# One transposition of 128x16 and four transfers for a unit's maxima, in place of four transpositions of 128x4 and one transfer

## Chip, cores and metric

The kernel runs on one core of one Trainium2 chip. The metric is the device time of one execution in microseconds; lower is better.

## What is computed

A gated block: 1024 query tokens (2 batches of 512, width 128) attend in 16 heads of 64 to 32 context tokens and to themselves, and a feed-forward layer of 8 experts follows, each token weighted to two of them. Only the attention matters here, cut to its core:

```
xn = layernorm(ctx, ...);  ln = layernorm(latents, ...)
q  = ln @ Wq
kv = concat([xn @ Wkv, ln @ Wkv])
qn = rmsnorm(q) * scale;   kn = rmsnorm(k)
sim  = einsum('bhid,bhjd->bhij', qn, kn)       # 544 keys a query: 32 context, 512 latents
attn = softmax(sim)                            # row maximum subtracted
out  = einsum('bhij,bhjd->bhid', attn, v) @ Wout + bout
```

## The kernel before

The attention is done in 8 **units** (u = 0 to 7), each one batch and a group of HG = 4 heads. A unit has 8 **slots**, so n = 0 to 63; slot n computes the turned scores (keys on partitions, 512 queries on the free axis) of one head and two of the four key tiles. Every engine has its own program, written out by slots from FIRST = -4 to LAST = 68, and semaphores join them. Numbers are kept in high and low halves of 16 bits, so most products come in pairs or triples.

Three things are needed of a unit before its slot 8u can start. (1) The **stacks** W1 and W2 (two buffers each, by u % 2): query and key halves laid one above the other, copied from HL by eight transfers on SyncE (L406 to L415) at slot 8u - 8, after the products of slot 8u - 9 or, for u = 1, at once. (2) The row **maxima**: score(j) on TensorE (L1381) computes the scores once with queries on partitions, VectorE reduces them to negated maxima (L991), joins them with the context's (L1072) and writes nm16, 128 queries on partitions by 4 query tiles and 4 heads. (3) The maxima must lie on the four partitions DH to M_ROWS = 64 to 67 of W2, one row a head, because the product of L1527 subtracts them by contracting with a one-hot block there. To get there, in slot 8u - 3 (nm_at) TensorE transposes nm16 into the bank o_ps[0] (turn_maxima, L1412), ScalarE copies it to nmT in SBUF (turned_maxima, L699), and in SyncE's slot 8u - 2 one transfer (L434) spreads nmT over the four places of the heads in W2. For unit 0 the same is done in the start-up. TensorE's slot 8u waits for w2_ok, sh_ok (the transfer of the maxima) and w1_ok.

SyncE's program between two units is: the maxima's transfer of unit u (slot 8u - 2), the eight transfers of the stacks of unit u + 1 (slot 8u, after the scores of slot 8u - 1), then for each of four heads three transfers of **pc_st** (L388, slot 8u + 1), which bring the context's exponentials of unit u into place; TensorE's times_values needs those of head 0 in slot 8u + 3 (L1362 with vst). SyncE further issues the experts' weights, 1 MB each: gate weights at slot 46 (L442) right behind unit 6's maxima, down weights at 51 (L445), up weights at 54 (L451) right behind unit 7's maxima. In the start-up SyncE issues unit 0's stacks, the maxima of unit 0, vst (six transfers, after vc), the stacks of unit 1 and pc_st of unit 0. ScalarE casts the experts' weights in quarters in slots 49 to 60 (SPLIT_AT: gate in 49 to 52, down in 53 to 56, up in 57 to 60).

Within a slot TensorE does the turned scores (L1526, L1527), one score(j) for a later unit, the projection and transposition of a later unit's query or key tile, the products with the values of slot n - 2 (times_values, L1356, L1357, L1362), and then, where it is due, turn_maxima. Unit 7 and half of 6 have projections of the output (L1333, L1316) in place of tiles.

Of the kernel before, what the change touches and what calls it, by code (L numbers as in the profile page):

```python
# [5 lines left out]
P = 128  # L6
F32 = mybir.dt.float32
F32R = mybir.dt.float32r
F16 = mybir.dt.float16
# [12 lines left out]
def flamingo_gated_block(nc, x, ctx_in, mask, g_xattn, g_ffn, ln_x_g, ln_x_b, ln_l_g, ln_l_b, qn_g, kn_g,  # L22
                         Wq, Wkv, Wout, bout, router, w_gate, w_up, w_down, out):
    B, N, D = x.shape
# [4 lines left out]
    HG = 4  # L29
# [13 lines left out]
    with ExitStack() as ctx:  # L43
# [79 lines left out]
        Vst = sb("vst", [3 * C, B, H, DH + 1], F16)  # L123
        nm_main = sb("nm_main", [P, 2, HG, QT], F32)
        nm16 = sb("nm16", [P, QT, HG], F16)
        nmT = sb("nmT", [HG, QT, P], F16)

        NP = 4
        p = [sb(f"p{k}", [P, 1024], F32) for k in range(NP)]
# [229 lines left out]
        @block.sync  # L359
        def _(sp):  # L360
            x_v = x.rearrange("b (t p) d -> p (b t) d", p=P)
            sp.dma_start(x_sb[:, 0:QT, :], x_v[:, 0:QT, :]).then_inc(x_in, 16)
            wq_v = Wq.rearrange("d (g c) -> d g c", g=NG)
            wkv_v = Wkv.rearrange("d (k g c) -> d k g c", k=2, g=NG)
            w_v = wqkv.rearrange("p (g k c) -> p g k c", g=NG, k=3)
            sp.dma_start(w_v[:, 0, 0, :], wq_v[:, 0, :]).then_inc(w0_in, 16)
            sp.dma_start(w_v[:, 0, 1:3, :], wkv_v[:, :, 0, :]).then_inc(w0_in, 16)
            sp.dma_start(x_sb[:, QT:T, :], x_v[:, QT:T, :]).then_inc(x_in2, 16)
            sp.dma_start(w_v[:, 1:NG, 0, :], wq_v[:, 1:NG, :]).then_inc(w_in, 16)
            sp.dma_start(w_v[:, 1:NG, 1, :], wkv_v[:, 0, 1:NG, :]).then_inc(w_in, 16)  # L370
            sp.dma_start(w_v[:, 1:NG, 2, :], wkv_v[:, 1, 1:NG, :]).then_inc(w_in, 16)
            for k, g in enumerate((qn_g, kn_g)):
                for r in range(2):
                    sp.dma_start(qk_gains[DH * r:DH * (r + 1), k:k + 1], g.unsqueeze(1)).then_inc(qkg_in, 16)
            sp.dma_start(mask_u8[:, :], mask.rearrange("b c -> (b c)").unsqueeze(0)).then_inc(mask_in, 16)
            for h in range(HG):
                sp.dma_start(mask_cu[C * h:C * (h + 1), :], mask.rearrange("b c -> c b"),
                             allow_slow_non_contiguous=True).then_inc(mask_in, 16)
            sp.dma_start(bout_b[:, :], bout.partition_broadcast(P)).then_inc(rest_in, 16)
            sp.dma_start(wr[:, :], router).then_inc(rest_in, 16)  # L380
            sp.dma_start(wout[:, :, :], Wout.rearrange("(c p) d -> p c d", p=P)).then_inc(rest_in, 16)

            def stack(u, h):

                for k, part in enumerate((pc_hi, pc_hi, pc_lo)):
                    if h == 0 and k == 2:
                        sp.wait_ge(cplo_ok, u + 1)
                    sp.dma_start(pc_st[u % 2][C * k:C * (k + 1), h, :], part[C * h:C * (h + 1), :]).then_inc(pcst_ok[h], 16)  # L388

            def slot(n):  # L390
                if n - 1 in cst_at:
                    u = cst_at[n - 1]
                    need(sp, pv_ok, 8 * (u - 1))
                    sp.wait_ge(cexp_ok, u + 1)
                    for h in range(HG):
                        stack(u, h)
                if n in W_AT:
                    u = W_AT[n]

                    need(sp, st_ok, 8 * (u - 1))  # L400
                    need(sp, cst_ok, u - 1)
                    sp.wait_ge(hi_ok, QT * (u + 1))
                    w1, w2, hl = W1[u % 2], W2[u % 2], HL[u % 2]
                    for odd in range(2):
                        rows = slice(DH * odd, DH * (odd + 1))
                        sp.dma_start(w1[0:DH, :, odd, :], hl[rows, 0, :, :]).then_inc(w1_ok[u % 2], 16)  # L406
                        sp.dma_start(w1[DH:P, 0:2, odd, :], hl[rows, 0, 0:2, :]).then_inc(w1_ok[u % 2], 16)
                    need_lo(sp, QT * (u + 1))
                    for odd in range(2):
                        rows = slice(DH * odd, DH * (odd + 1))  # L410
                        sp.dma_start(w1[DH:P, 2:4, odd, :], hl[rows, 1, 2:4, :]).then_inc(w1_ok[u % 2], 16)
                    for odd in range(2):
                        rows = slice(DH * odd, DH * (odd + 1))

                        sp.dma_start(w2[0:DH, :, odd, :], hl[rows, :, :, :].rearrange("p a c n -> p (a c) n")[:, 2:6, :]  # L415
                                     ).then_inc(w2_ok[u % 2], 16)
                if n == FIRST:
                    sp.wait_ge(cklo_ok, 1)
                    for odd in range(2):
                        rows = slice(DH * odd, DH * (odd + 1))  # L420
                        for k, part in ((K1c[0:DH], 0), (K1c[DH:P], 1), (K2c[0:DH], 0)):
                            sp.dma_start(k[:, :, odd, :], kc_hl[rows, part, :, :]).then_inc(kc_ok, 16)
                if n == -1:
                    sp.wait_ge(const_z, 4)
                    sp.wait_ge(cvlo_ok, 1)
                    for b in range(B):
                        for k, cols in enumerate((slice(0, DH + 1), slice(DH + 1, VW), slice(0, DH + 1))):
                            sp.dma_start(Vst[C * k:C * (k + 1), b, :, 0:cols.stop - cols.start],
                                         vc[b * C:(b + 1) * C, :, cols]).then_inc(vbd_ok, 16)
                if n - 1 in nm_at:  # L430
                    u = nm_at[n - 1]
                    sp.wait_ge(nmc_ok, u + 1)

                    sp.dma_start(W2[u % 2][DH:M_ROWS, 2:4, :, :].rearrange("p a e n -> p (a e) n"),  # L434
                                 nmT[:, :, :].rearrange("p q c -> p (q c)").unsqueeze(1).broadcast_to([HG, HG, N])
                                 ).then_inc(sh_ok[u % 2], 16)

                if n == 46:
                    sp.wait_ge(w2_ok[0], 32 * (UNITS // 2))
                    sp.wait_ge(w1_ok[0], 96 * (UNITS // 2))  # L440
                    sp.wait_ge(s_ok, 8 * (UNITS - 1))
                    sp.dma_start(wg.rearrange("p (e f) -> p e f", e=E), w_gate.rearrange("e d f -> d e f")).then_inc(wg_in, 16)  # L442
                if n == 51:
                    sp.wait_ge(pv_ok, 8 * 6)
                    sp.dma_start(wd.rearrange("p (e c d) -> p e c d", e=E, c=FC),  # L445
                                 w_down.rearrange("e (c p) d -> p e c d", p=P)).then_inc(wd_in, 16)
                if n == 54:
                    sp.wait_ge(w2_ok[1], 32 * (UNITS // 2))
                    sp.wait_ge(w1_ok[1], 96 * (UNITS // 2))
                    sp.wait_ge(s_ok, 8 * UNITS)  # L450
                    sp.dma_start(wu.rearrange("p (e f) -> p e f", e=E), w_up.rearrange("e d f -> d e f")).then_inc(wu_in, 16)  # L451

            for n in range(FIRST, LAST):
                slot(n)
            out_v = out.rearrange("b (t p) d -> p (b t) d", p=P)
            for half in range(B):
                if half == 0:
                    sp.wait_ge(yp_ok, E)
                else:
                    sp.wait_ge(y_ok, E * QT)  # L460
                sp.dma_start(out_v[:, half * QT:(half + 1) * QT, :], x1[:, half * QT:(half + 1) * QT, :]).then_inc(out_ok, 16)
            sp.wait_ge(out_ok, 16 * B)
# [185 lines left out]
        def _(act):  # L648
# [46 lines left out]
            def turned_maxima(u):  # L695
                act.wait_ge(nmT_ok, u + 1)
                if u:
                    act.wait_ge(sh_ok[(u - 1) % 2], 16 * ((u - 1) // 2 + 1))
                nc.scalar.copy(nmT[:, :, :], o_ps[0][0:HG, 0:256].bitcast(F16).rearrange("p (q c) -> p q c", c=P)  # L699
                               ).then_inc(nmc_ok, 1)  # L700

            weights_hi(0)
            act.wait_ge(gains_in, 16 * 4)
# [567 lines left out]
        def _(pe):  # L1271
# [136 lines left out]

            def turn_maxima(u):
                pe.wait_ge(nm_ok, u + 1)  # L1410
                for q in range(QT):
                    last = nc.tensor.transpose(o_ps[0][0:HG, 64 * q:64 * (q + 1)].bitcast(F16), nm16[:, q, :],  # L1412
                                               ident_h[:, :])
                last.then_inc(nmT_ok, 1)

            pe.wait_ge(wlo_ok, 1)
            pe.wait_ge(lnlo_ok, 2)
# [92 lines left out]
            def turned_scores(n):  # L1510
                u, h, i = n // 8, n % 8 // 2, n % 2
                if n % 8 == 0:
                    pe.wait_ge(w2_ok[u % 2], 32 * (u // 2 + 1))
                    pe.wait_ge(sh_ok[u % 2], 16 * (u // 2 + 1))
                    pe.wait_ge(w1_ok[u % 2], 96 * (u // 2 + 1))
                if n == 0:
                    pe.wait_ge(onehot_ok, 2)
# [177 lines left out]
```

## Time and profile before

| | |
|---|---|
| three runs | 346.26 us median, 345.56 to 347.9 |
| the profiled execution | 347.66 us, of which its span 345.9 us |
| TensorE busy | 301.0 us, 87% of the span |
| VectorE, GpSimd, ScalarE busy | 79%, 78%, 59% |
| granted TensorE clock, mean of the span | 0.975 |

Up to about 55 us the kernel starts up (norms, weights split into halves, the first two units' queries and keys); 55 to about 260 us are the slots; from there to the end the experts run, paced by GpSimd. A view of the trace gives times in us from the start of the span. PE is TensorE, PEld its weight loads, DVE VectorE, ACT ScalarE, POOL GpSimd, SP SyncE; a q behind a name is the engine's own sequencer, which issues transfers. L numbers are lines of the kernel. Durations of matrix products overlap, since they are pipelined.

### The profile page before, as it was taken

To read this page: it belongs to the slowest core of one execution; us is meant where nothing else is said; L and a number is where in the kernel's file an instruction comes from. 1 tells how busy PE (TensorE), PEld (TensorE's weight loads), DVE (VectorE), ACT (ScalarE), POOL (GpSimd) and SP (SyncE) were. 2 spreads that over 40 slices of the span, in tenths; PEclk is the share of its full clock that TensorE was granted. 3 is DMA by queue.
4 is the path that set the end of the run, shared out by engine and by line. 5 is a ranking of instruction groups with operands and counts; after the bars stand their busy time and mean duration, and the time that the engine had idled before them with its cause. 6 is when DMAs were issued, how large, how long until landed. Compare 5 with 4: busy or idle time off the path is not lost.

```text
span 345.9 us, 8714 instructions
## 1 busy us (share of the span) xinstructions
PE 301.0 (87%) x3321; PEld 184.3 (53%) x3321; DVE 273.5 (79%) x515; ACT 204.9 (59%) x357; POOL 268.0 (78%) x203
## 2 busy tenths in 40 slices
PE   0566578789999999999999999999987898988992
PEld 0233243446555555555555656788764674654652
DVE  3898878958899899898988976955647885887994
ACT  2463746727756757665766656467662657554551
POOL 8689896866999999999989987565971475875562
PEclk9996969989999999999999999999999999999999
DMA  6505322810712614416307259450100000001001
GB/s 165 151 1 127 69 35 44 193 39 17 174 45 49 152 36 107 106 23 148 69 20 164 60 154 181 112 165 9 38 2 3 2 1 0 2 3 31 2 0 33
DMA packets 33708, 23.63 MB, mean 68 GB/s; under 512 B 10818, under 2 KB 33154, under 8 KB 33666
## 3 DMA queue, kind: packets, MB, share of 16 engines
q1 hardware_dynamic: 32722, 23.03, 28.8%
q8 instruction: 27, 0.44, 0.6%
q10 hardware_dynamic: 944, 0.04, 0.2%
q14 instruction: 15, 0.12, 0.1%
HBM read 5.87 MB, written 0.52 MB: 18 GB/s over the span
## 4 chain that ended last, share of the span: by engine, by line
PE 53%; POOL 16%; issue 11%; ACT 5%; DVE 5%; SPq 4%; DMA 4%; POOLq 0%; DVEq 0%; ACTq 0%
POOL p_lo L628 9%; PE big L1526 7%; PE big L1527 7%; PE o_ps L1362 5%; PE big L1381 5%; PE o_ps L1356 4%; PE o_ps L1357 4%; DMA pc_st<-pc_lo 3%; PE tv L1369 3%; POOL rms_r L492 3%; PE pj L1333 2%; PE pj L1292 2%; PE pj L1293 1%; PE pj L1294 1%; POOL x_sb L641 1%
## 5 line engine op out<-in xcount | busy, mean ns | idle before, releaser
L593 POOL TENSOR_TENSOR p_lo<-p 128x1024 f16<-128x1024 f32 x64 | 121.8, 1915 | 13.1 <-ACT p L792 13.1
L792 ACT ACTIVATE p<-big 128x1024 f32<-128x1024 f32 x64 | 65.6, 1025 | 48.9 <-PE big L1527 48.8
L991 DVE TENSOR_REDUCE nm_main<-big 128x2 f32<-128x1024 f32 x64 | 78.2, 1222 | 18.1 <-PE big L1381 17.3
L492 POOL TENSOR_TENSOR rms_r<-meansq,power 128x8 f32<-128x8 f32 x32 | 52.3, 1637 | 16.1 <-DVE meansq L965 16.1
L628 POOL TENSOR_TENSOR p_lo<-p,p_lo 128x512 f16<-128x512 f32 x32 | 37.0, 1158 | 25.9 <-ACT p_lo L865 25.9
L1526 PE MATMUL big<-w 128*128 128x512 f16 x128 | 48.8, 381 | 1.9 <-ACT p L792 1.6
L1527 PE MATMUL big<-w 68*128 68x512 f16 x128 | 48.7, 380 | 0.0
L1356 PE MATMUL o_ps<-v,p 128*128 128x65 f16 x512 | 40.7, 194 | 0.0
L1357 PE MATMUL o_ps<-v,p 128*128 128x64 f16 x512 | 40.6, 195 | 0.0
L1356 PEld LDWEIGHTS o_ps<-v,p 128*128 128x128 bf16 x512 | 35.9, 99 | 6.7 <-issue 3.6
L1357 PEld LDWEIGHTS o_ps<-v,p 128*128 128x128 bf16 x512 | 34.4, 98 | 3.2
L860 ACT ACTIVATE p<-big 128x512 f32<-128x512 f32 x32 | 19.1, 598 | 23.4 <-PE big L1617 23.3
L1381 PE MATMUL big<-hl 64*128 64x512 f16 x128 | 25.8, 400 | 5.8 <-DVE nm_main L991 4.9
L1236 DVE SCALAR_TENSOR_TENSOR p<-p,big 128x512 f32<-128x512 f32 x32 | 21.9, 684 | 11.4 <-ACT p L860 10.9
L1636 PE MATMUL o_ps<-wd_hi,p_lo 128*128 128x128 f16 x128 | 23.2, 220 | 6.4 <-POOL p_lo L628 6.4
L1362 PE MATMUL o_ps<-v,p_lo 128*128 128x65 f16 x512 | 26.1, 194 | 0.0
L965 DVE TENSOR_REDUCE meansq<-squares 128x8 f32<-128x512 f32 x32 | 21.9, 683 | 5.4 <-ACT squares L670 4.7
L1615 PE MATMUL big<-x2T_hi,gu_hi 128*128 128x512 f16 x64 | 24.3, 379 | 2.0 <-DVE p L1240 2.0
L1617 PE MATMUL big<-x2T_hi,wqkv_hl 128*128 128x512 f16 x64 | 24.3, 379 | 0.0
L1616 PE MATMUL big<-x2T_lo,gu_hi 128*128 128x512 f16 x64 | 24.3, 379 | 0.0
L1381 PEld LDWEIGHTS big<-hl 64*128 64x128 f16 x128 | 6.2, 93 | 32.8 <-issue 25.5
L1640 PE MATMUL o_ps<-wd_hi,p_lo 128*128 128x128 f16 x128 | 23.1, 219 | 0.0
(228 smaller groups left out, 715.6 us busy)
## 6 DMA issues: line engine op xcount, KB each, us to landing
w<-hl SPq DMA_DIRECT2D x32, 256.0 KB, 4.2
w<-hl SPq DMA_DIRECT2D x32, 128.0 KB, 3.7
pc_st<-pc_hi SPq DMA_DIRECT2D x64, 32.0 KB, 1.9
pc_st<-pc_lo SPq DMA_DIRECT2D x32, 32.0 KB, 1.9
hl<-n_kernel_gating_EDF_dram SPq DMA_DIRECT2D x1, 1024.0 KB, 6.5
hl<-L_ffn_kernel_up_EDF_dram SPq DMA_DIRECT2D x1, 1024.0 KB, 5.5
o_sb<-in_L_xattn_Wkv_dram SPq DMA_DIRECT2D x2, 384.0 KB, 7.2
x_sb<-in_x_dram SPq DMA_DIRECT2D x2, 256.0 KB, 3.7
```

What stands on the lines that cost most here:

```text
L492: nc.gpsimd.tensor_tensor(rms_r[:, tau % QT, :], meansq[:, tau % QT, :], power[:, 0:8], ALU.pow).then_inc(rr_ok, 1)
L593: nc.gpsimd.tensor_tensor(p_lo[m % NP][:, :], p[m % NP][:, :], p_hi[m % NP], ALU.subtract).then_inc(plo_ok, 1)
L628: nc.gpsimd.tensor_tensor(hid_lo[m % NH], hid[m % NH], hid_hi[m % NH], ALU.subtract).then_inc(hlo_ok, 1)
L792: nc.scalar.activation(p[n % NP][:, :], st_ps, ACT.Exp).then_inc(exp_ok, 1)
L991: nc.vector.tensor_reduce(nm_main[:, u % 2, 2 * c:2 * c + 2, q], s2_ps.rearrange("p (k n) -> p k n", k=2), AX_X, ALU.max, negate=True).the ...
L1356: nc.tensor.matmul(o_of(q), ph[:, c], vh, start=start and q == 0, stop=False, skip_group_check=True)
L1357: nc.tensor.matmul(o_of(q)[:, 0:DH], ph[:, c], vl, start=False, stop=False, skip_group_check=True)
L1362: last = nc.tensor.matmul(o_of(q), pl[:, c], vh, start=False, stop=True, skip_group_check=True)
L1381: last = nc.tensor.matmul(s2_ps[:, 512 * r:512 * (r + 1)], HL[u % 2][rows, 0, c, q * P:(q + 1) * P], HL[u % 2][rows, 0, 2 + c, :], start=T ...
L1526: nc.tensor.matmul(o, w1[:, 2 + h // 2, h % 2, keys], w1[:, h // 2, h % 2, :], start=True, stop=False)
L1527: last = nc.tensor.matmul(o, w2[0:M_ROWS, h // 2, h % 2, keys], w2[0:M_ROWS, 2 + h // 2, h % 2, :], start=False, stop=True)
L1615: nc.tensor.matmul(o, gu_hi[k][:, w], x2T_hi[:, toks], start=True, stop=False)
```

## The change

A unit's maxima are turned by one transposition of 128x16 (128 queries by 4 tiles x 4 heads) into 16 partitions by 128 columns. ScalarE copies 16x128 in place of 4x512. The rows of query tile q now lie on partitions 4q to 4q + 3, while W2 wants all four tiles of a head on one partition, so SyncE issues four transfers, one a query tile, each with rows of 128 numbers (256 bytes) instead of 512 (1024 bytes). All waits on sh_ok count four times 16.

```diff
-        nmT = sb("nmT", [HG, QT, P], F16)
+        nmT = sb("nmT", [QT * HG, P], F16)
...
-                    sp.dma_start(W2[u % 2][DH:M_ROWS, 2:4, :, :].rearrange("p a e n -> p (a e) n"),
-                                 nmT[:, :, :].rearrange("p q c -> p (q c)").unsqueeze(1).broadcast_to([HG, HG, N])
-                                 ).then_inc(sh_ok[u % 2], 16)
+                    for q in range(QT):
+                        sp.dma_start(W2[u % 2][DH:M_ROWS, 2:4, :, q * P:(q + 1) * P].rearrange("p a e n -> p (a e) n"),
+                                     nmT[q * HG:(q + 1) * HG, :].unsqueeze(1).broadcast_to([HG, HG, P])
+                                     ).then_inc(sh_ok[u % 2], 16)
...
-                    act.wait_ge(sh_ok[(u - 1) % 2], 16 * ((u - 1) // 2 + 1))
-                nc.scalar.copy(nmT[:, :, :], o_ps[0][0:HG, 0:256].bitcast(F16).rearrange("p (q c) -> p q c", c=P)
-                               ).then_inc(nmc_ok, 1)
+                    act.wait_ge(sh_ok[(u - 1) % 2], 16 * QT * ((u - 1) // 2 + 1))
+                nc.scalar.copy(nmT[:, :], o_ps[0][0:QT * HG, 0:P // 2].bitcast(F16)).then_inc(nmc_ok, 1)
...
-                for q in range(QT):
-                    last = nc.tensor.transpose(o_ps[0][0:HG, 64 * q:64 * (q + 1)].bitcast(F16), nm16[:, q, :],
-                                               ident_h[:, :])
-                last.then_inc(nmT_ok, 1)
+                nc.tensor.transpose(o_ps[0][0:QT * HG, 0:P // 2].bitcast(F16), nm16[:, :, :].rearrange("p q h -> p (q h)"),
+                                    ident_h[:, :]).then_inc(nmT_ok, 1)
...
-                    pe.wait_ge(sh_ok[u % 2], 16 * (u // 2 + 1))
+                    pe.wait_ge(sh_ok[u % 2], 16 * QT * (u // 2 + 1))
```

On TensorE, in the start-up where unit 0's maxima are turned (between the transposition of a key tile and the projection of the context's values), the difference is this:

```order
 L1294 MATMUL pj<-wqkv_hl,lnT_lo 128x512
 L1369 MATMUL o_ps<-ident,qk 128x128 x4
-L1412 MATMUL o_ps<-ident_h,nm 4x128 x4
+L1411 MATMUL o_ps<-ident_h,nm 16x128
 L1292 MATMUL big<-wqkv_hl,lnT_hi 128x256
 L1293 MATMUL big<-wqkv_hl,lnT_hi 128x256
```

Four transpositions became one, in the same place; the same stands in each of the other seven units. On SyncE, in slots 46 to 48 (the maxima of unit 6, then the gate weights as hl, then the stacks of unit 7; lines behind 434 are numbered one higher after the change), it is this:

```order
 L388 DMA pc_st<-pc_hi 32x512 x2
 L388 DMA pc_st<-pc_lo 32x512
-L434 DMA w_0<-nmT 4x4x512
-L442 DMA hl<-L_ffn_kernel_gating_EDF_dram 128x8x256
+L435 DMA w_0<-nmT 4x4x128 x4
+L443 DMA hl<-L_ffn_kernel_gating_EDF_dram 128x8x256
 L406 DMA w_1<-hl 64x4x512
 L407 DMA w_1<-hl 64x2x512
```

The order of SyncE's transfers is kept; four issues stand where one stood, ahead of whatever follows.

## Rows read from the trace of the kernel before

**Rows 1.** The page: granted clock in 40 slices of 8.65 us; the chain by engine.

```profile
PEclk9996969989999999999999999999999999999999
...
PE 53%; POOL 16%; issue 11%; ACT 5%; DVE 5%; SPq 4%; DMA 4%; POOLq 0%; DVEq 0%; ACTq 0%
```

**Rows 2.** The chain in order of time, start-up: start us, us, what.

```profile
49.77 0.51 PE o_ps L1412 x4
...
51.68 0.21 PE big L1292
...
52.20 0.11 PE big L1292
...
54.94 0.65 SPq L428
...
55.64 0.63 SPq L428
...
67.76 2.95 DMA pc_st<-pc_lo
```

**Rows 3.** Waits of TensorE, whole span, then from 86 to 260 us: total, times, longest.

```profile
PE o_ps L1362 <- DMA pc_st<-pc_lo: 2.9, 3, 1.9
...
PE o_ps L1362 <- DMA pc_st<-pc_lo: 1.0, 2, 0.7
```

**Rows 4.** Busy time of each engine in the stretch 86 to 110 us.

```profile
86.00:110.00 24.00, 24.00 (x312) 13.93 (x309) 21.43 (x37) 15.84 (x26) 23.34 (x15) 1.00 0.38 84
```

**Rows 5.** The chain in unit 2: the four transpositions for unit 3.

```profile
128.36 0.32 PE o_ps L1412 x4
```

**Rows 6.** Lines 699 and 434 (duration min/median/max, first and last start); ScalarE's copies from PSUM.

```profile
L699 ACT COPY nmT<-o_ps x8: 557/574/575, 50.4 to 225.1; 4x512 f16<-4x512 f16 x8
...
L434 SPq DMA_DIRECT2D w<-nmT x8: 706/716/793, 51.0 to 225.7; - x8
...
L766 ACT COPY o_sb<-tv 128x512 f32<-128x512 f32 x16 | 9.4, 586 | 15.9 <-PE tv L1316 15.9
...
L693 ACT COPY p_lo<-o_ps 128x256 f32<-128x256 f32 x4 | 1.5, 372 | 0.0
```

**Rows 7.** Timeline of SyncE and TensorE, units 1 and 2; DMA rate in slices of 0.1 us from 105.

```profile
81.33 0.71 SPq L434 DMA_DIRECT2D w<-nmT  x1
...
86.22 0.38 PE L1526 MATMUL big<-w 128*128 128x512 f16 x1
...
105.14 0.71 SPq L434 DMA_DIRECT2D w<-nmT  x1
108.64 0.67 SPq L406 DMA_DIRECT2D w<-hl  x1
...
110.39 0.38 PE L1526 MATMUL big<-w 128*128 128x512 f16 x1
...
GB/s 0 0 0 0 0 0 0 0 0 0 0 0 0 0 10 20 31 31 20 21 21 10 82 0 0 0 0 0 0 0 0 0 0 0 0 0 0 0 0 0
```

**Rows 8.** The chain at unit 6's pc_st; line 388, durations of its issues.

```profile
212.93 4.25 DMA pc_st<-pc_lo
...
L388 SPq DMA_DIRECT2D pc_st<-pc_lo x32: 507/590/1937, 67.8 to 248.1; - x32
```

**Rows 9.** Timeline of SyncE and TensorE before unit 6.

```profile
201.25 0.72 SPq L434 DMA_DIRECT2D w<-nmT  x1
202.08 0.39 SPq L442 DMA_DIRECT2D hl<-n_kernel_gating_EDF_dram  x1
...
205.53 0.38 PE L1526 MATMUL big<-w 128*128 128x512 f16 x1
```

**Rows 10.** DMA busy tenths, 203 to 219 us (0.4 a slice), 248 to 252 (0.1), and its last landing.

```profile
DMA  3778999999999999999999999998841410303213
...
DMA  3630001640000561000000000000000000000000
...
pc_st<-pc_lo SPq DMA_DIRECT2D x1, 32.0 KB, 1.8
```

## Prediction

> **What bounds the kernel now.** I read the page's slices and its chain of work first, then the chain stretch by stretch, then SyncE's queue, because the change works on TensorE, ScalarE and SyncE together. The chain is 53% TensorE and 16% GpSimd; SyncE's queue has 4% and DMA 4% [rows 1]. By stretch it looks like this.
>
> From 49.77 to 70.84 us the start-up is bound first by TensorE (the four transpositions stand in it with 0.51 us), then by ScalarE and VectorE on vc, then by SyncE alone: fifteen transfers are issued one behind the other from 54.94 us, and the last thing waited for is the landing of the first head's pc_st [rows 2]. TensorE has then stood idle for 1.9 us, its longest wait for pc_st [rows 3]. From there to unit 6 TensorE is the bound: from 86 to 110 us it is busy 24.00 of 24.00 us, GpSimd 23.34 of them, VectorE 21.43 [rows 4]. A unit repeats every 24.17 us (slot 16's first product at 110.39, slot 8's at 86.22 [rows 7]). In unit 6 the chain leaves TensorE: it runs over SyncE's issues of pc_st and a landing 4.25 us after the third of them at 212.93 [rows 8]. The same happens more weakly in unit 7: of TensorE's three waits for pc_st, 2.9 us in all, two lie behind 86 us, with 1.0 us together and 0.7 the longer [rows 3]. Behind that come the experts, which the change does not touch.
>
> **What the change takes away.** (a) *Three of four transpositions per unit, on TensorE.* Four occupy 0.32 us of the chain in a full unit [rows 5]; they are pipelined, 0.08 us apart, so one leaves 0.08 and saves 0.24 us. In unit 0 four cost 0.51 us [rows 2], because the granted clock is still low there: the PEclk row reads 6 in the sixth slice, 43.2 to 51.9 us [rows 1], and products of 256 columns take 0.21 us up to 51.9 us, which is 1.2 GHz, and 0.11 us behind it, which is 2.4 GHz [rows 2]. One would save 0.38 us; but if the clock rises at the same instant as now, 0.38 us more of the work is done at half speed, and half the gain is given back. I take 0.3 us, bounds 0.2 and 0.4.
>
> (b) *ScalarE's copy.* It takes 574 ns for 4x512 [rows 6]. I have no 128-column copy from PSUM. A COPY of 512 columns takes 586 ns and one of 256 takes 372 ns, so 0.84 ns a column, and 128 columns would be 0.27 us; the bound from above is the 256-column copy itself. I take 0.27, by the slope of two rows of this operation: the copy ends 0.30 us sooner (0.20 at least). ScalarE is not in the chain here, so this is worth nothing by itself; it only brings the transfers forward. Together with (a) the first transfer is issued 0.54 us sooner.
>
> **What it adds.** (c) *Three more issues on SyncE per unit.* One nmT issue takes 716 ns [rows 6], and issues in a row stand 0.04 to 0.05 us apart [rows 2]. So the fourth is issued 3 x 0.76 = 2.28 us behind the first, and what SyncE does next can start 2.28 us later, less the 0.54 us. Where does that go?
> - Unit 0: the issue began at 51.0 us and took at most 0.79; SyncE then idled until 54.94 [rows 2, 6]. 3.1 us of cover against 1.7: nothing. Without that cover it would be 1.7 us straight on the chain, as everything from 54.94 to 67.76 us is SyncE issuing.
> - Units 1 to 5: unit 2's issue ended at 105.85, the next one (the stacks of unit 3) waits for slot 15's scores until 108.64 [rows 7]. Cover 2.79 against 1.7: nothing.
> - Unit 6: SyncE issues the 1 MB gate weights (L442) at 202.08, right behind nmT [rows 9]. They now go out at 202.08 - 0.54 + 2.28, so 1.74 us later against everything around. The stacks of unit 7 queue up behind them.
> - Unit 7: the up weights (L451) go out 1.7 us later, in slot 54, and are cast in slots 57 to 60 at the earliest, three slots of 3 us on. Nothing.
>
> (d) *The landing.* TensorE's first product of slot 8u waits for all four. No view gives a landing for nmT, so I work it out. In unit 2 packets flow at 10 to 31 GB/s in slices 15 to 22 of 0.1 us from 105.0 (the 82 GB/s in the next one I take for something else), which is 1.3 to 2.1 us after the issue [rows 7]. pc_st's semaphore comes 0.3 us behind its last packet (the last one is issued at 248.1, its packets run until 249.6, it lands after 1.8 [rows 8, 10]). So a transfer is there 2.4 us after its issue; a quarter of the bytes can shorten only the 0.7 us in which packets flow. The fourth lands 2.28 + 2.4 = 4.7 us behind the first issue, 4.2 if small packets are quick. Available are, from the first issue to the first product of the slot, 86.22 - 81.33 = 4.89 us in unit 1, 110.39 - 105.14 = 5.25 in unit 2 (and 5.24 in 3 to 5), 205.53 - 201.25 = 4.28 in unit 6 [rows 7, 9], each plus the 0.30 us of the copy. So the slack is 0.5 us in unit 1, 0.85 in units 2 to 5, and -0.1 to +0.4 in unit 6. I take 0.05 us of waiting, in unit 6 alone. In unit 0 the wait may reach 0.3 us, but TensorE has 1.9 us to give away there [rows 3].
>
> Four transfers overlap in this sum. pc_st's are issued 0.63 us apart and its bursts in the DMA row lie 0.6 us apart too [rows 10], so they do. The Trainium skill (DMA: Bandwidth & Descriptors, Rules for kernel authors) speaks against the change: many small transfers should be coalesced into one large, since under 64 KB one pays mostly overhead. The same page's section Anatomy of one DMA gives about 2 us of fixed cost to each. By a reading in which that cost falls due four times in a row, the time would be the serial rival's below; by the row it falls due once.
>
> (e) *The gate weights in unit 6.* This is the term that I am least sure of. From 203.4 to 214.6 us the DMA engines read 7 to 9 tenths: the gate weights, then unit 7's stacks, then pc_st [rows 10]. The first head's pc_st ends behind that queue, at 217.18 us, and TensorE has then been idle 0.7 us [rows 3, 8]. If the queue starts 1.74 us later and nothing else gives, TensorE resumes 1.74 us later. But the row thins out at 214.6 us, 2.6 us before that landing, and single issues of pc_st stall, up to 1.94 us where 0.59 is usual [rows 8]; that tail need not move along. Bounds 0 and 1.74; I take 1.2, nearer to the full shift because the saturated stretch is four times as long as the tail.
>
> **The sum.** Unit 0: -0.3. Units 1 to 5, where TensorE is full: 5 x -0.24 = -1.2. Unit 6: its own 0.24 only lengthens its wait, +1.2 for (e), +0.05 for (d). Unit 7: -0.24. Together -0.5 us, on a profiled execution of 345.9 us of span and 347.66 us in all. The median of the three runs is 346.26, 1.4 below that execution; the difference goes onto the median: **345.8 us**.
>
> **Rivals.**
> - *The gate weights hide (0.10).* If (e) is 0, and the wait of 0.3 us in unit 7 goes too, -0.4 - 1.2 - 0.24 - 0.3 = -2.1: **344.1**. For it: the thin tail. Against it: eleven busy microseconds before.
> - *GpSimd takes over (0.14).* It is busy 23.34 of 24.00 us [rows 4], so only 0.66 us of air stands in a unit; the waits between it and TensorE could eat the 0.24 us. Then -0.3 + 1.2 - 0.2 is +0.7: **347.0**.
> - *Late staging, the slower side (0.06).* If a transfer of 256-byte rows needs over 3.3 us from issue to landing (5.25 + 0.30 - 2.28), slot 8u begins late in every unit, and TensorE has no slack to give back. At 4.3 us it is 1.0 us in units 2 to 5, 1.4 in unit 1 and 1.9 in unit 6: +7.3, so **353**. For it: single issues of up to 1.94 us occur [rows 8]; one of those among the four costs a unit up to 0.5 us. Against it: the packets of today are done 2.1 us after the issue.
> - *Serial transfers (0.02).* If each began when the one before had landed, the fourth would land 4 x 2.4 = 9.6 us behind the first issue, 4.1 us late in each of units 2 to 5, 4.4 in unit 1, 5.0 in unit 6: +25, **371**. The pc_st rows speak against it.
>
> My forecast keeps 0.68. **Range 343.9 to 348.6**: the low end is the first rival; the high end is (e) in full (+1.74 instead of 1.2), no gain by (a) in unit 0, GpSimd eating most of the five units, and one stall of SyncE of 0.7 us between 54 and 68 us, where it is the chain. About 1% (3.5 us) is what a measurement of this kernel can tell from no change. Faster by more than that needs 342.8, which the first rival would have to overshoot: 0.02, taken from it. Slower needs 349.7, which only the last two reach: 0.08. Same keeps 0.90.
>
> **What would show it.** (a) one transposition of 128*16, 0.08 us in the chain, units 24.17 - 0.24 = 23.9 us apart (slot 16 less slot 8, first products). (b) the copy near 270 ns. (c) four issues 0.76 us apart, no later start of the stacks except in unit 6, where L443 comes 2.8 us behind nmT's first. (d) no DMA named as what ended an idle time before the first product of slots 8, 16, 24, 32, 40. (e) TensorE's wait for pc_st in unit 6 grows from 0.7 to about 2.1 us. I am wrong if that wait stays where it is, if the unit's period stays at 24.17, or if the first product of slot 8u waits for w.

## The result, and the profile after

The changed kernel takes 348.90 us (median of 20 runs, 345.18 to 351.0), the kernel before 346.61 beside it (20 runs, 345.55 to 348.14). The ratio is 1.0053, interval 1.0036 to 1.007: about 1.8 us slower, by the medians 2.3. I had forecast 345.8 and a range up to 348.6. So the median lies 0.3 us outside the range, and the sign is wrong. It is still within the 1% that I called the same.

The profiled execution takes 349.32 us, its span 347.2 (345.9 before), its mean granted clock is 0.963 (0.975 before). The traces therefore differ by 1.3 us, less than the medians do.

To see where, I read the start of a unit's first product (slot 8u) from the timelines, and that of slot 63.

| first product of slot (us) | before | after | difference |
|---|---|---|---|
| 0 | 54.99 | 54.57 | -0.42 |
| 8 | 86.22 | 85.62 | -0.60 |
| 16 | 110.39 | 109.63 | -0.76 |
| 40 | 182.87 | 181.60 | -1.27 |
| 48 | 205.53 | 204.10 | -1.43 |
| 56 | 232.64 | 234.39 | +1.75 |
| 63 | 255.06 | 256.37 | +1.31 |
| end of the span | 345.9 | 347.2 | +1.3 |

The change gains 0.17 us in every full unit (24.17 us a unit before, 24.00 after) and is 1.43 us ahead at slot 48. Of the 0.60 us at slot 8 only the 0.17 for unit 1's transposition is the change's doing, as far as the traces show: slot 8 begins anywhere from 83.5 to 87.0 us in the nine traces of kernels with the one transposition, so the start-up's gain in this pair is the luck of two executions (see the last section). Between slots 48 and 56 it loses 3.18 us: that stretch takes 27.11 us before and 30.29 after. Unit 7 gives back 0.44. The sum is -0.60 - 0.83 + 3.18 - 0.44 = +1.31 us. The question is what the 3.18 us are.

The page's clock row and its chain by engine, after (the same views as [rows 1]):

```profile
PEclk9996859989999999999999999899999999999998
...
PE 53%; POOL 16%; issue 10%; SPq 7%; DVE 5%; ACT 5%; DMA 3%; POOLq 0%; DVEq 0%; ACTq 0%
```

SyncE's queue has grown from 4 to 7% of the chain, and slice 26 of 40 (217 to 225.7 us) reads 8 where it read 9.

Now the chain around unit 6, in order of time (start us, us, what; answers [rows 5, 8]):

```profile
127.60 0.15 PE o_ps L1411
...
199.03 0.17 PE o_ps L1411
199.22 0.26 ACT nmT L700
199.50 0.71 SPq L435
...
202.45 0.40 SPq L443
...
203.32 0.68 SPq L406
...
212.21 5.37 DMA pc_st<-pc_lo
217.62 0.30 PE o_ps L1362 x4
...
219.58 0.43 PE big L1524
...
224.98 0.21 PE big L1524
```

The chain now leaves TensorE at the transposition for unit 6 itself. It runs through ScalarE's copy and all four issues of the maxima (L435) to the gate weights (L443), then over the stacks (L406) to the landing of pc_st. Before, it stayed on TensorE until unit 6 itself and left it only at 209.48 us, for ScalarE's context exponentials (the line below) and two issues of L388. The landing takes 5.37 us where it took 4.25. The two lines at the end show the second thing: a product of 512 columns occupies 0.43 us at 219.58 and 0.21 at 224.98. These are the two levels of the granted clock, 1.2 and 2.4 GHz. From the chain before:

```profile
210.21 0.68 ACT pc_hi L806
```

SyncE's and TensorE's timelines before unit 6 (start us, us, what; answers [rows 9]):

```profile
199.50 2.83 SPq L435 DMA_DIRECT2D w<-nmT  x4
202.45 0.40 SPq L443 DMA_DIRECT2D hl<-n_kernel_gating_EDF_dram  x1
...
204.10 0.38 PE L1524 MATMUL big<-w 128*128 128x512 f16 x1
...
217.62 0.30 PE L1362 MATMUL o_ps<-vst,pc_st 96*128 96x65 f16 x4 [2.56 <-DMA pc_st<-pc_lo]
```

Against the first product of slot 48 the gate weights went out 3.45 us early before (205.53 - 202.08) and 1.65 us early after: 1.80 us later, where I had said 1.74. The wait in brackets, TensorE idle until pc_st landed, is 2.56 us and was 0.73. That leaves 3.18 - 1.83 + 0.17 (unit 7's saved transpositions, which stand in slot 53) = 1.5 us that is no wait at all. It is in the clock. TensorE in two windows behind that wait after the change, and in one before it (stretch, its length, busy time of PE, PEld, DVE, ACT, POOL with counts, granted clock, DMA share, GB/s). After:

```profile
217.80:218.80 1.00, 1.00 (x13) 1.00 (x10) 0.00 (x0) 0.00 (x0) 0.03 (x1) 1.00 0.26 62
219.40:221.40 2.00, 2.00 (x7) 0.53 (x5) 1.00 (x4) 1.18 (x3) 0.00 (x0) 0.50 0.15 31
```

Before:

```profile
219.20:221.20 2.00, 2.00 (x30) 1.08 (x28) 1.86 (x7) 1.79 (x3) 0.13 (x1) 1.00 0.21 53
```

TensorE is busy in all three, but at half the clock in the second. (The counts, 7 and 30, are not the factor: the two windows hold products of different lengths.) The cleanest measure is the work from the product that ends the wait (217.62 after, 217.22 before) to the first product of slot 53 (224.81 and 222.87): the same instructions take 7.19 us where they took 5.65. The clock is still full in the first microsecond of work behind the wait; it is at half from 218.93 to 222.34 us.

The rest of the change reads as forecast, by line (durations min/median/max, first and last start, shape):

```profile
L1411 PE MATMUL o_ps<-ident_h,nm x8: 222/223/277, 49.5 to 226.6; 128*16 128x128 f16 x8
...
L700 ACT COPY nmT<-o_ps x8: 237/254/254, 50.2 to 226.9; 16x128 f16<-16x128 f16 x8
...
L435 SPq DMA_DIRECT2D w<-nmT x32: 637/660/797, 50.5 to 229.4; - x32
```

### The profile page after: what moved, and what is told of

It is laid out like the page before. It is cut to its first block, busy times and chain, and to the rows that moved or that the text cites. A ratio compares the mean times of both kernels' runs of the same rounds, so it can differ in the third digit from the quotient of the medians.

```text
span 347.2 us, 8690 instructions
## 1 busy us (share of the span) xinstructions
PE 301.6 (87%) x3297; PEld 184.2 (53%) x3297; DVE 269.6 (78%) x515; ACT 202.3 (58%) x357; POOL 268.5 (77%) x203
## 4 chain that ended last, share of the span: by engine, by line
PE 53%; POOL 16%; issue 10%; SPq 7%; DVE 5%; ACT 5%; DMA 3%; POOLq 0%; DVEq 0%; ACTq 0%
POOL p_lo L629 9%; PE big L1524 7%; PE big L1525 7%; PE o_ps L1362 5%; PE big L1381 5%; PE o_ps L1356 4%; PE o_ps L1357 4%; PE pj L1333 3%; PE tv L1369 3%; DMA pc_st<-pc_lo 2%; POOL rms_r L493 2%; PE pj L1292 2%; PE pj L1294 1%; PE pj L1293 1%; PE tv L1316 1%
## 5 line engine op out<-in xcount | busy, mean ns | idle before, releaser
L792 ACT ACTIVATE p<-big 128x1024 f32<-128x1024 f32 x64 | 65.5, 1024 | 51.4 <-PE big L1525 51.4
L1634 PE MATMUL o_ps<-wd_hi,p_lo 128*128 128x128 f16 x128 | 23.2, 220 | 6.4 <-POOL p_lo L629 6.4
L1636 PE MATMUL o_ps<-wqkv_hl,p_lo 128*128 128x128 bf16 x128 | 23.1, 219 | 0.0
```

Source lines behind the costliest of these rows:

```text
L792: nc.scalar.activation(p[n % NP][:, :], st_ps, ACT.Exp).then_inc(exp_ok, 1)
```

## Experiments

Each experiment's ratio is against the kernel before on the same chip, whose medians there were 346.78 (e1, e2, e3, e5), 346.62 (e4, e6, e7, e8) and 346.15 us (e9, e10).

### The gate weights ahead of the maxima (e1)

Does the loss come from the gate weights' queue, or from the four transfers themselves? The changed kernel, with the 1 MB issued in front of unit 6's four transfers instead of behind them (it then needs one wait more, for cs_ok):

```diff
+                if n == 46:
+                    sp.wait_ge(w2_ok[0], 32 * (UNITS // 2))
+                    sp.wait_ge(w1_ok[0], 96 * (UNITS // 2))
+                    sp.wait_ge(s_ok, 8 * (UNITS - 1))
+                    sp.wait_ge(cs_ok, UNITS - 1)
+                    sp.dma_start(wg...., w_gate....).then_inc(wg_in, 16)
                 if n - 1 in nm_at:
...
-                if n == 46:
-                    sp.wait_ge(w2_ok[0], 32 * (UNITS // 2))
...
```

> The changed kernel with one edit: SyncE issues the gate weights of slot 46 ahead of unit 6's maxima, not behind their four transfers. Theory A (the loss sits in unit 6: the gate weights leave late, the queue that pc_st stands in ends late, TensorE waits 2.56 us and its clock falls to 1.2 GHz behind the wait): the wait for pc_st falls below 0.8 us, no stretch at 0.5 follows, and the time is the kernel before less the gain of units 0 to 5, 346.6 - 1.5 = about 345. Theory B (four transfers cost something in every unit, whatever the weights do): it stays at 348.4, within 0.7.

Measured: 345.70 us, ratio 0.9971, interval 0.9952 to 0.9991. SyncE's timeline of e1:

```profile
198.17 0.61 SPq L435 DMA_DIRECT2D hl<-n_kernel_gating_EDF_dram  x1
...
200.71 3.15 SPq L441 DMA_DIRECT2D w<-nmT  x4
```

and TensorE's waits for pc_st over the whole span (total, times, longest):

```profile
PE o_ps L1363 <- DMA pc_st<-pc_lo: 2.4, 1, 2.4
```

That single wait is the start-up's; the one in unit 6 is gone. The stretch from slot 48 to 56 takes 26.28 us instead of 30.29. The edit does more than give the 1.8 us back: the weights leave 7.14 us ahead of slot 48, where even the kernel before had 3.45, and with it the 0.73 us that the kernel before itself waited is gone as well. The four transfers are still issued one by one, 2.5 us behind the weights, and cost nothing. So the loss is what stands behind them in SyncE's queue in unit 6.

### Four transfers alone (e2)

The kernel before with its four transpositions and its 4x512 copy, but four transfers of 128 columns each (the waits for them count accordingly, here and in e3 and e5):

```diff
-                    sp.dma_start(W2[u % 2][DH:M_ROWS, 2:4, :, :]....,
-                                 nmT[:, :, :]....broadcast_to([HG, HG, N])
-                                 ).then_inc(sh_ok[u % 2], 16)
+                    for q in range(QT):
+                        sp.dma_start(W2[u % 2][DH:M_ROWS, 2:4, :, q * P:(q + 1) * P]....,
+                                     nmT[:, q, :].unsqueeze(1).broadcast_to([HG, HG, P])
+                                     ).then_inc(sh_ok[u % 2], 16)
```

> The kernel before with its four transpositions and its copy of 4x512, but the staging filled by four transfers of 128 columns in place of one. Theory A: no gain of 0.17 us a unit, so all of unit 6's loss is seen: wait for pc_st about 3 us, the clock stretch behind it, 3.4 us lost less 0.4 us that the vanished wait of unit 7 gives back: 349.6. Theory B' (the transposition or the copy of 16 partitions is the costly part): 346.6 as before.

Measured: 350.21 us, ratio 1.0097, interval 1.0075 to 1.012. The slot 8 to slot 48 stretch is 119.32 us, as in the kernel before (119.31), so five full units do not feel the three extra issues. Slot 48 to 56 is 29.66 us, 2.55 more than before. The size came out (3.4 us by the ratio, 3.0 expected), but not by the way I expected. TensorE's and ScalarE's timelines of e2 in unit 6:

```profile
217.76 0.30 PE L1363 MATMUL o_ps<-vst,pc_st 96*128 96x65 f16 x4 [1.44 <-DMA pc_st<-pc_lo]
...
230.27 0.62 ACT L847 CAST wd_hi<-v 128x512 f16<-128x512 f32 x1 [2.50 <-DMA v<-ffn_kernel_down_EFD_dram]
...
231.87 0.39 PE L1527 MATMUL big<-w 128*128 128x512 f16 x1 [1.70 <-ACT p L793]
```

The wait for pc_st is 1.44 us, not 3, and the clock does not fall. Instead the next 1 MB, the down weights, arrives late: ScalarE's cast waits 2.50 us for it, and TensorE waits 1.70 us for ScalarE. So the cost of a later queue moves: it comes out at the context's exponentials in one trace and at the down weights in another.

### One transfer in place of four (e3 and e5)

The changed kernel, but the copy of rows for a unit done by a single transfer, which spreads tile 0's maxima over all four tiles. The softmax then subtracts another value than the row's maximum; the bytes and places are the same. e3 does it in all eight units, e5 in unit 6 alone (`if u == 6`):

```diff
-                    for q in range(QT):
-                        sp.dma_start(W2[u % 2][DH:M_ROWS, 2:4, :, q * P:(q + 1) * P]....,
-                                     nmT[q * HG:(q + 1) * HG, :].unsqueeze(1).broadcast_to([HG, HG, P])
-                                     ).then_inc(sh_ok[u % 2], 16)
+                    if u >= 0:                                  # e5: u == 6
+                        sp.dma_start(W2[u % 2][DH:M_ROWS, 2:4, :, :]....,
+                                     nmT[0:HG, :]....broadcast_to([HG, HG * QT, P])
+                                     ).then_inc(sh_ok[u % 2], 16)
...
```

> The changed kernel with its one transposition and 16x128 copy, but a single transfer, which puts query tile 0's maxima under all four tiles (part of the result is therefore another). Bytes and packets are as in the changed kernel. Theory A: the gains of units 0 to 5 (1.4 us) and of the earlier issue stay and nothing is lost in unit 6: 346.6 - 1.8 = 344.8, wait for pc_st at or below 0.7 us. Theory B': as slow as the changed kernel, 348.4.

> The changed kernel with four transfers in seven units and a single one (tile 0's maxima under all four tiles, so part of the result is another) in unit 6 alone. Theory A (all of the cost is in unit 6): the same as with a single transfer in every unit, 344.8, within 0.4 us. Theory B (cost spread over the units): 348.4 less a seventh of the loss, 347.9.

Measured: e3 346.23 us (343.16 to 348.44), ratio 0.9964, interval 0.9936 to 0.9991. e5 344.65 us (343.64 to 347.43), ratio 0.9955, interval 0.9932 to 0.9979. The intervals cover each other, and the spans are 341.4 and 342.3 us. Slot 8 to 48 is 118.48 us in both and in the changed kernel, slot 48 to 56 is 26.32 and 26.89. Four transfers in seven units cost nothing that can be measured; in unit 6 they are the whole loss. e5's wait for pc_st in unit 6:

```profile
213.68 0.30 PE L1370 MATMUL o_ps<-vst,pc_st 96*128 96x65 f16 x4 [0.69 <-DMA pc_st<-pc_lo]
```

It is 0.69 us, close to the kernel before's 0.73, with the one transposition in place. How much such a landing scatters is seen in e3, whose unit 6 is written like e5's and has no wait for pc_st at all. e3 is the half of the change that gains by itself: its whole interval lies below 1, though by its ratio it gains 1.2 us, not the 1.8 expected.

### Other work of TensorE ahead of the wait (e4)

Is the wait for pc_st the mechanism, or only a mark of it? In the changed kernel, slot 51 does the projection and transposition of an output tile before the products with the values instead of behind them, so that TensorE has work while pc_st travels:

```diff
+                if n == 51:
+                    project_o(TURN_AT[n - 1])
+                    turn_o(TURN_AT[n])
                 if is_slot(n - 2):
...
-                if n - 1 in TURN_AT:
+                if n - 1 in TURN_AT and n != 51:
...
-                if n in TURN_AT:
+                if n in TURN_AT and n != 51:
```

> The changed kernel with TensorE's order in slot 51 altered: the projection and transposition of the output (12 instructions, about 1.4 us, which need nothing of pc_st) stand ahead of the products that wait for pc_st, not behind them. Theory A: the wait shrinks from 2.56 to about 1.15 us; if the clock holds at that length both the 1.4 us and the 1.5 us of the slow stretch come back, 348.4 - 2.9 = 345.5; if it falls all the same, 347.0. Theory B: 348.4.

Measured: 346.25 us, ratio 0.9998, interval 0.9975 to 1.0021. TensorE's timeline and a window of e4 behind its wait (columns as above):

```profile
216.65 0.30 PE L1362 MATMUL o_ps<-vst,pc_st 96*128 96x65 f16 x4 [1.26 <-DMA pc_st<-pc_lo]
...
219.40:221.40 2.00, 2.00 (x23) 1.75 (x21) 2.00 (x3) 0.31 (x1) 1.45 (x1) 1.00 0.73 219
```

The wait is 1.26 us instead of 2.56, the clock stays at 1.00, and the stretch from slot 48 to 56 is 27.44 us, against 27.11 in the kernel before. The queue is as late as in the changed kernel (the gate weights leave 1.66 us ahead of slot 48); only the hole in TensorE is smaller. That gives back nearly all of the loss in unit 6. In time e4 is 1.9 us below the changed kernel by their ratios, where I had expected 2.9.

### Idle products in the wait (e8, e9, e10)

How much of the 3.18 us is the clock? In e8 the changed kernel fills the wait with 24 products of 128x128 that nobody reads. They delay nothing that has arrived, since TensorE would stand still there:

```diff
+    FILL = 24
...
+                    if u == 6 and h == 0:
+                        for _ in range(FILL):
+                            nc.tensor.matmul(pj[:, 3 * P:4 * P], ident_h[:, :], ident_h[:, :], start=True, stop=True,
+                                             skip_group_check=True)
                     pe.wait_ge(pcst_ok[h], 48 * (u + 1))
```

> The changed kernel with 24 idle products of 128x128 (into a part of the bank pj that nobody reads then) ahead of TensorE's wait for unit 6's first pc_st, about 1.9 us of work that lies inside the wait of 2.56 us. Nothing that anyone waits for moves. Clock theory (part of the loss is the granted clock that falls behind an idle TensorE): no stretch at 0.5 behind the wait, 1.5 us come back, 346.9. Rival (the slow stretch has another cause, or costs nothing in the end): 348.4.

Measured: 347.42 us, ratio 1.0033, interval 1.0008 to 1.0059. TensorE's timeline of e8 and the window behind the wait:

```profile
213.80 1.50 PE L1507 MATMUL pj<-ident_h 128*128 128x128 f16 x24
...
216.39 0.30 PE L1363 MATMUL o_ps<-vst,pc_st 96*128 96x65 f16 x4 [1.09 <-DMA pc_st<-pc_lo]
...
219.40:221.40 2.00, 2.00 (x40) 1.72 (x37) 2.00 (x2) 0.76 (x1) 1.16 (x1) 1.00 0.60 155
```

Filler and wait are 1.50 + 1.09 = 2.59 us, as long as the 2.56 us of pure waiting, yet the clock does not fall. From the product that ends the wait to the first product of slot 53 (222.03) e8 takes 5.64 us, like the kernel before (5.65), where the changed kernel takes 7.19. The fall costs 7.19 - 5.65 = 1.54 us. From the first product of slot 51 to that of slot 53 it is 8.59 us in the kernel before and 11.96 in the changed one, 3.37 more: the 1.54 and the 1.83 by which the wait grew.

e8 came out at 347.42 against an expected 346.9, and it was not timed beside the changed kernel. I therefore ran the unaltered changed kernel (e9) and e8 again (e10) on one chip:

> The changed kernel once more, unaltered, beside the kernel with the filler below, on one chip. It gives a second trace. Clock theory: the wait for unit 6's first pc_st is 2.3 to 2.6 us again; the granted clock falls to 0.5 behind it for some 3.4 us in this trace too if the fall follows from the idle time alone, and not if it also depends on where the wait lies in time. Median 348.4.

> The kernel with 24 idle products inside the wait once more. Clock theory: no granted clock of 0.5 behind the wait of unit 6, and a median 0.7 to 1.7 us below that of the changed kernel of the same job. Rival (the clock's fall is worth nothing in the end): medians equal within 0.5 us.

Measured: e9 348.95 us, ratio 1.0054, interval 1.0021 to 1.0086; e10 347.02 us, ratio 1.0038, interval 1.001 to 1.0065. e9's trace:

```profile
217.71 0.29 PE L1362 MATMUL o_ps<-vst,pc_st 96*128 96x65 f16 x4 [2.29 <-DMA pc_st<-pc_lo]
...
219.40:221.40 2.00, 2.00 (x8) 0.56 (x5) 1.08 (x4) 1.11 (x3) 0.00 (x0) 0.50 0.19 46
```

The slowdown is there again (1.0053 and 1.0054), with a wait of 2.29 us and the same fall of the clock; in e10 the wait is 0.73 us behind the filler and the clock stays. Slot 48 to 56 takes 30.02 us in e9 and 28.25 in e10. From the end of the wait to slot 53 it is 7.19 us in e9 and 5.65 in e10, the same figures as in the first pair. The medians of e9 and e10 differ by 1.9 us, but their ratios by only 0.16%, 0.6 us, and the intervals overlap. So the fall and its price of 1.54 us are shown in two pairs of traces; what the filler gains in the timed runs is not: the estimates go from 0.6 to 1.9 us, and no gain at all is not excluded.

Does the place of the wait decide, and not its length? In the changed kernel and in e9 it ends at the same place of the span (217.62 and 217.71), so this pair cannot tell. But e2's wait ends there too, at 217.76, is 1.44 us long, and no fall follows.

### Both kernels with unit 6 mended (e6 and e7)

The edits of e1 and e4 together, once on the changed kernel (e6) and once on the kernel before (e7): the gate weights' block stands ahead of the maxima, the output's work ahead of the waiting products. This asks what the change is worth where nothing waits for pc_st in unit 6.

```diff
+                if n == 46:
+                    sp.wait_ge(w2_ok[0], 32 * (UNITS // 2))
...
+                if n == 51:
+                    project_o(TURN_AT[n - 1])
+                    turn_o(TURN_AT[n])
```

> The changed kernel with the gate weights ahead of the maxima in slot 46 and the output's work ahead of the waiting products in slot 51. Theory A: no wait for pc_st is left in unit 6, 346.6 - 1.8 = 344.8 or a little below.

> The kernel before with the same two edits as the one above (gate weights ahead of the maxima, output's work ahead in slot 51). It says what the change under study is worth once unit 6 is out of the way. Theory A: 346.6 - 0.7 (its own wait for pc_st) = 345.9, so the version with one transposition and four transfers is faster by the 1.2 to 1.4 us of units 0 to 7.

Measured: e6 343.64 us (six runs, 342.91 to 344.86), ratio 0.993, interval 0.9908 to 0.9951; e7 345.99 us, ratio 0.9994, interval 0.9974 to 1.0014. TensorE's waits for pc_st in the whole span, e6 and then e7:

```profile
PE o_ps L1363 <- DMA pc_st<-pc_lo: 0.3, 1, 0.3
```

```profile
PE o_ps L1363 <- DMA pc_st<-pc_lo: 0.7, 1, 0.7
```

Neither waits for pc_st in unit 6. Between them the change is worth 345.99 - 343.64 = 2.35 us, about 2.2 by the ratios, where I had expected 1.2 to 1.4. e6 beats both kernels: 2.4 us below the kernel before, by its ratio. e7 is no better than the kernel before, and its trace shows where unit 6 gives the gain back. From slot 51 to 53 e7 takes 7.68 us instead of 8.59, from slot 53 to 56 10.56 instead of 9.77. There ScalarE's cast waits 1.44 us for the down weights, and TensorE for ScalarE:

```profile
227.79 0.39 PE L1527 MATMUL big<-w 128*128 128x512 f16 x1 [0.65 <-ACT p L793]
```

e6 takes 9.58 us there, without such a wait; its down weights leave 14.59 us behind slot 48, e7's 15.37. So of the 2.5 us between the spans of e6 and e7 some 0.8 us is the landing of the down weights, in one trace of each, and not what the transpositions save; and 0.6 us lies in the start-up already. Why those weights leave later in e7 stays open.

## Why the prediction was wrong, point by point

**(a) Three of four transpositions: right in kind, smaller in the units.** One stands in the chain with 0.15 to 0.17 us, not 0.08: what I divided by four was a pipelined row of four, and a single one costs more than its quarter. The period fell by 0.17 us (24.17 to 24.00), not by 0.24, so five units gave -0.83 instead of -1.2. For the start-up I had 0.3 us at slot 0 and 0.54 at slot 8, and this pair has 0.42 and 0.60. That agreement is luck. Unit 0's first product with pc_st, which ends the start-up's wait, begins at 69.9 to 71.7 us in the nine traces with one transposition and at 70.7 to 70.8 in the three with four: no gain in unit 0 is shown. By slot 48 my terms come to -1.74, and the trace has -1.43.

**(b) The copy: right.** 254 ns, forecast 270. (A slip of mine beside it: the issues from 54.94 us to the first head's last pc_st transfer are seventeen, not fifteen. Nothing was worked out from the number.)

**(c) Three more issues: right.** The four take 2.83 us and L443 begins 2.95 us behind the first; I had said 2.8. The 1.74 us came out (1.80) by two errors that cancel. The three more issues shift L443 by 2.95 - 0.83 = 2.12 us, not 2.28. And against slot 48 the first issue is only 0.32 us sooner (4.60 us ahead of it, before 4.28), not 0.54, because the transposition's gain brings slot 48 forward too. The covers held: outside unit 6 no stack is late. e2 (119.32 against 119.31 us for slots 8 to 48) and e5 show it.

**(d) The landing: right.** No transfer is named before the first product of slots 8 to 48. It is in unit 0, where the trace has 0.30 us:

```profile
54.57 0.38 PE L1524 MATMUL big<-w 128*128 128x512 f16 x1 [0.30 <-DMA w<-nmT]
```

That was the bound I gave, and it was time that TensorE has to give: it waits 1.9 us for pc_st later in the start-up, as before. The wait ends 4.11 us behind the first issue (50.46), where I had 4.2 to 4.7. The transfers of unit 2 overlap, as the DMA rate shows in slices of 0.1 us from 104 (first issue at 104.07; compare the last line of [rows 7]):

```profile
GB/s 0 0 0 0 0 0 0 0 0 0 0 0 0 0 21 18 3 0 0 0 0 15 21 5 0 82 0 0 15 15 10 0 0 0 0 23 18 0 0 0
```

Four bursts about 0.7 us apart begin 1.3 us behind the first issue, the last ending 3.6 us behind it. The Trainium skill (DMA: Bandwidth & Descriptors, Anatomy of one DMA) charges about 2 us of fixed cost to a transfer, in a section on transfers issued from GpSimd; these are issued from SyncE, and the bursts show that here no such cost is paid four times in a row. The Trainium skill's advice to coalesce small transfers (DMA: Bandwidth & Descriptors, Rules for kernel authors) nevertheless gave the right sign, though not for the overhead that it names: what counted was the three issues that stand ahead of the next large transfer. e5 is 344.65 with one transfer there.

**(e) The gate weights in unit 6: the step that failed.** In this term I priced TensorE's longer wait by its length alone and put the work behind it at full clock, without a reason. In the changed kernel the wait of 2.56 us is followed by 3.4 us at 1.2 GHz, and that is 1.54 us on top, which stood in no term, no rival and no bound. The rows that I had in hand showed such a fall: the kernel before waits 1.9 us for pc_st in the start-up, until 70.84 us [rows 2, 3], and the ninth slice of its clock row, 69.2 to 77.8 us, reads 8 [rows 1]. In the chain before, products of 512 columns take 0.22 us just behind that wait and 0.43 from 72.4 us on:

```profile
71.12 0.22 PE big L1526
...
72.32 0.41 PE pj L1292
72.73 0.43 PE pj L1293
```

I read that wait as time that TensorE could give away, and did not look at the clock behind it.

The other half of (e) is a matter of size. I had the wait grow from 0.7 to about 2.1 us (+1.2, and the transposition's 0.24); it grew by 1.83. My argument for less, "that tail need not move along", did not hold. Measured from slot 48, the busy stretch of the DMA engines ends at 9.1 us before (214.6) and at 10.9 after (215.0, to a slice of 0.4), and from there to pc_st's landing it is 2.6 us in both. The DMA row after, 203 to 219 us, 0.4 a slice:

```profile
DMA  0166799889999999999999999999995541112303
```

But one pair of traces does not fix that size. With the same issues ahead, pc_st is 1.3 to 1.9 us later than in the kernel before in e4, e8, e9 and e10, and only 0.7 in e2.

**The sum, redone with what the pair of traces shows** (us, in the terms of the forecast):

| term | forecast | traces |
|---|---|---|
| unit 0 | -0.3 | -0.43, luck of the start-up |
| units 1 to 5 | -1.2 | -0.83 |
| unit 6, the wait, less its own transposition | +1.2 | +1.83 - 0.17 = +1.66 |
| unit 6, the clock behind the wait | none | +1.54 |
| unit 6, landing of the maxima | +0.05 | 0 |
| unit 7, its transposition and the rest of the way to slot 56 | -0.24 | -0.19 |
| unit 7, slots 56 to 63 | none | -0.44 |
| together | -0.5 | +1.31 |

The last line but one stood only in my first rival: unit 7's wait of 0.3 us for pc_st is gone. The timed difference is 1.8 us by ratio and 2.3 by medians, more than the 1.31. Leave the start-up out, and the traces agree better with it: from slot 8 to the end of the span they are 259.7 us before and 261.6 after, 1.9 more. So the pair's lucky start-up is the likely reason why its spans differ by less than the timed runs do; it is not shown.

**The rivals.** *The gate weights hide* fell: the wait grew. *GpSimd takes over* fell: the period went down with the transpositions, and so it did in e1, e3 and e5 (118.48 us for slots 8 to 48 in each). Its time, 347.0, was the nearest of the rivals, for a wrong reason. *Late staging* and *serial transfers* fell: no unit's first product waits. That unit 6's wait costs more than its length was in no rival, though the profile before had the sign of it.

The range failed by the same term. Its upper end took the wait in full but no price beyond it.

## What to carry to other kernels

When an edit adds issues to a queue, ask what the largest transfer behind them is and who waits at its end; the 4 KB transfers cost nothing in seven units, and 1.8 us of delay of 1 MB cost 3.4 us in the eighth. Price a longer wait of TensorE by its length and by the clock behind it, and look at the granted clock after the wait, not in it; a wait of like length elsewhere in the profile before may show it already. A saving of a few tenths per unit is worth taking once the place is mended where it is paid for: e6 has the change, the large transfer first and other work ahead of the wait, and has the lowest median of all.

## What the hardware showed that I had not expected

**The clock falls behind a wait, not at it.** In unit 6, waits of 0.69, 0.73, 1.09, 1.26 and 1.44 us (e5, before, e8, e4, e2) were followed by full clock, and so was e2's wait of 1.70 us at 231.87; waits of 2.29 and 2.56 us (e9, after) were followed by 0.50. The fall comes 1.3 us after work has resumed and lasts 3.4 us. With 1.50 us of idle products in the wait it did not come (e8, e10). The start-up has the same in six traces (before, after, e1, e2, e9, e10): TensorE waits 1.83 to 2.39 us for pc_st until about 71 us, and 1.2 to 1.75 us after it has resumed the clock is at half for 3.4 us. No length of a wait is shown from which on the clock falls: TensorE is less busy ahead of that wait (7.22 of 8.90 us from 60.0 to 68.9 in the kernel before) than in unit 6 (11.40 of 11.40 from 205.0 to 216.4). The Trainium skill (TensorE: Matmul & The Clock Gate, Part 1) gives 1.2 GHz as the clock of an idle engine and 2.4 of a busy one. The levels agree with this trace (0.43 and 0.21 us for 512 columns); that the lower one is met while TensorE is busy again is what the rows add.

**A start-up that falls either way.** e8 and e10 are the same kernel, but slot 8 begins at 84.51 us in e8 and at 86.97 in e10. In e8 the clock is at half from 59.85 to 63.26 us, ahead of the wait for the first pc_st. That slows work that would have been done early in any case, and the wait is 0.23 us. In e10 the wait is 2.39 us, and the clock is at half from 72.95 to 76.37, behind it. One window of each, e8 and then e10:

```profile
60.00:63.00 3.00, 3.00 (x17) 1.19 (x15) 1.67 (x3) 1.34 (x3) 1.20 (x2) 0.50 0.69 130
```

```profile
73.00:75.50 2.50, 2.28 (x10) 1.42 (x10) 1.32 (x2) 1.55 (x2) 0.00 (x0) 0.50 0.22 53
```

The twelve traces divide in the same way. From unit 0's first product with pc_st to slot 8, the kernels with one transposition take 15.21 to 15.24 us where the half clock lies behind that product (after, e1, e9, e10), and 13.65 to 13.66 us where it lies ahead of it (e3, e4, e5, e6, e8). With four transpositions it is 15.38 (before, e2) and 13.82 (e7). The difference, 1.56 us, is the price of such a fall once more, beside the 1.54 in unit 6; the other 0.9 us between e8 and e10 is a later landing. Runs of one kernel spread over 2 to 6 us; this is one source of it that the traces show. What decides where the clock falls stays open.
